# Two more rounding-correction terms in both activation quantizers of a feed-forward sublayer on eight cores

## The reference, cut to what matters

```
def act_quant(x):
    scale = 127.0 / jnp.clip(jnp.max(jnp.abs(x), axis=-1, keepdims=True), 1e-05)
    return jnp.clip(jnp.round(x * scale), -128, 127) / scale
def weight_quant(w):
    scale = 1.0 / jnp.clip(jnp.mean(jnp.abs(w)), 1e-05)
    return jnp.clip(jnp.round(w * scale), -1, 1) / scale
def bit_linear(x, w):        # the value is that of the quantized operands
    return jnp.einsum('bsd,hd->bsh', act_quant(x), weight_quant(w))
...
h = bit_linear(x, w1)                        # 1024 -> 4096
h = silu(depthwise_conv1d(h, conv_w, conv_b))   # 3 taps along the tokens
return bit_linear(h, w2)                     # 4096 -> 1024
```

## Time and profile before

| | |
|---|---|
| time, median of 3 runs | 10609.23 us (10607.76 to 10616.51) |
| the profiled execution: its own time | 10610.17 us |
| its span (slowest core, first to last instruction) | 10608.6 us |
| spans of the 8 cores | 10564.5 to 10608.6 us |
| VectorE busy | 3761.9 us, 35% |
| TensorE busy | 3693.5 us, 35% |
| ScalarE busy | 1905.7 us, 18% |

### The profile page before, as it was taken

The page is one execution under the profiler, slowest core; times in us unless marked ns, Lnnn a source line. Parts: engine busy times, 40 slices in busy tenths (PEclk is TensorE's granted clock), DMA queues, the critical chain, the costliest instruction groups (busy, mean ns, idle before and its releaser), DMA issues.

```text
span 10608.6 us, 72542 instructions; the slowest of 8 cores (10564.5 to 10608.6 us)
## 1 busy us (share of the span) xinstructions
PE 3693.5 (35%) x21474; PEld 2012.1 (19%) x21474; DVE 3761.9 (35%) x6202; ACT 1905.7 (18%) x3771; POOL 0.2 (0%) x4
## 2 busy tenths in 40 slices
PE   3333333400002334443343343333334414433343
PEld 1111111100001222222211111121111102222232
DVE  2111111123357655666411111111111176666655
ACT  1333333000000000000123333333333100000000
POOL 0000000000000000000000000000000000000000
PEclk9555555655555666666665555555555556666666
DMA  1000000032211334333100000000000003333344
GB/s 53 4 4 8 4 5 12 30 97 75 74 51 38 64 75 80 79 80 68 42 2 4 4 1 4 4 1 4 4 4 1 16 2 73 77 79 64 64 86 97
DMA packets 1187213, 407.74 MB, mean 38 GB/s; under 512 B 1129236, under 2 KB 1162264, under 8 KB 1186840
## 3 DMA queue, kind: packets, MB, share of 16 engines
q1 hardware_dynamic: 1186840, 403.11, 17.0%
HBM read 377.88 MB, written 25.17 MB: 38 GB/s over the span
## 4 chain that ended last, share of the span: by engine, by line
PE 30%; DVE 25%; DMA 17%; issue 13%; ACT 10%; DVEq 4%; SPq 1%; ACTq 0%; POOLq 0%
PE ps L43 26%; DVE FQ L43 11%; DMA W1TS<-w1t 7%; DMA WPF<-w 5%; ACT PPBb L43 4%; DVE HQ L43 4%; DVEq L43 3%; DMA W2TS<-w2t 3%; PE pt L43 2%; ACT PPBa L43 2%; DVE LCOL L43 1%; ACT TMPB L43 1%; PE pss L43 1%; DVE TMPA L43 1%; DVE SR L43 1%
## 5 line engine op out<-in xcount | busy, mean ns | idle before, releaser
L43 PE MATMUL ps<-HQ,W2TS 128*128 128x256 bf16 x4096 | 559.5, 304 | 1288.1 <-DVEq L43 1177.9
L43 PE MATMUL ps<-XQT,W1TS 128*128 128x258 bf16 x4096 | 832.1, 376 | 491.1 <-DMA W1TS<-w1t 462.5
L43 PE MATMUL ps<-VBb,PPAb 128*128 128x129 bf16 x2048 | 482.9, 297 | 1003.7 <-ACT PPBb L43 1003.7
L43 DVE RECIPROCAL LCOL<-ps 128x3 f32<-128x3 f32 (+2 forms) x160 | 28.9, 180 | 1982.1 <-PE ps L43 1966.5
L43 PEld LDWEIGHTS ps<-HQ,W2TS 128*128 128x128 bf16 x4096 | 437.1, 109 | 1398.7 <-issue 1308.5
L43 PE MATMUL pt<-CID,TMPB 128*128 128x128 bf16 (+1 forms) x1408 | 183.2, 279 | 1362.9 <-DVEq L43 983.2
L43 PEld LDWEIGHTS ps<-XQT,W1TS 128*128 128x128 bf16 x4096 | 492.8, 128 | 826.0 <-issue 666.0
L43 ACT ACTIVATE PPAb<-ps,LCOL 128x384 bf16<-128x384 f32 (+1 forms) x768 | 418.2, 545 | 995.4 <-PE ps L43 994.8
L43 ACT ACTIVATE TMPB<-ps 128x256 bf16<-128x256 f32 (+1 forms) x192 | 87.3, 454 | 2635.4 <-PE ps L43 2635.4
L43 DVE SCALAR_TENSOR_TENSOR FQ<-ps,CONVP,FQ 128x256 f32<-128x256 f32 x1024 | 495.4, 484 | 82.3 <-issue 6.9
L43 PE MATMUL ps<-VBb,PPBb 128*128 128x129 bf16 x2048 | 519.4, 315 | 0.0
(11 more groups left out here) (139 smaller groups left out, 5491.8 us busy)
## 6 DMA issues: line engine op xcount, KB each, us to landing
W1TS<-w1t SPq DMA_DIRECT2D x512, 256.0 KB, 3.1
W2TS<-w2t SPq DMA_DIRECT2D x128, 1024.0 KB, 7.6
WPF<-w SPq DMA_DIRECT2D x128, 512.0 KB, 4.1
WSAa<-wqkv SPq DMA_DIRECT2D x24, 512.0 KB, 3.9
X<-x SPq DMA_DIRECT2D x1, 8192.0 KB
w1t<-WTS SPq DMA_DIRECT2D x32, 256.0 KB, 2.8
w2t<-WTS SPq DMA_DIRECT2D x32, 256.0 KB, 2.8
out<-X SPq DMA_DIRECT2D x1, 8192.0 KB, 22.0
```

Source lines behind the costliest of these rows:

```text
L43: r = f(*a, **k)
```

## The change

It adds terms to both rounding corrections and touches nothing else. In `qq`, after the comparisons with 0.5, it adds those with 1.5 and 2.5 on either side: four operations over 1024 columns and two drains for each token tile. In `qz` it adds the comparison with 2.5 on either side: two operations over 2048 columns and two drains for each piece, four pieces a chunk. All of it is VectorE work, in place on tiles that exist already; no wait, semaphore, load or matmul is added or moved.

```diff
@@ qq, for each of 16 token tiles
                 v.tensor_single_scalar(FQ[:, 3072:4096], FQ[:, 2048:3072], -0.5,
                                        OP.is_lt)
                 v.drain()
+                v.scalar_tensor_tensor(FQ[:, 0:1024], FQ[:, 2048:3072], 1.5,
+                                       FQ[:, 0:1024], OP.is_gt, OP.add)
+                v.scalar_tensor_tensor(FQ[:, 3072:4096], FQ[:, 2048:3072], -1.5,
+                                       FQ[:, 3072:4096], OP.is_lt, OP.add)
+                v.drain()
+                v.scalar_tensor_tensor(FQ[:, 0:1024], FQ[:, 2048:3072], 2.5,
+                                       FQ[:, 0:1024], OP.is_gt, OP.add)
+                v.scalar_tensor_tensor(FQ[:, 3072:4096], FQ[:, 2048:3072], -2.5,
+                                       FQ[:, 3072:4096], OP.is_lt, OP.add)
+                v.drain()
                 v.tensor_sub(FQ[:, 1024:2048], FQ[:, 0:1024], FQ[:, 3072:4096])
@@ qz, for each of four pieces of a chunk
                     v.scalar_tensor_tensor(B, A, 1.5, B, OP.is_gt, OP.add)
                     v.drain()
+                    v.scalar_tensor_tensor(B, A, 2.5, B, OP.is_gt, OP.add)
+                    v.drain()
                     v.tensor_single_scalar(Ho, A, -0.5, OP.is_lt)
                     v.drain()
                     v.scalar_tensor_tensor(Ho, A, -1.5, Ho, OP.is_lt, OP.add)
+                    v.drain()
+                    v.scalar_tensor_tensor(Ho, A, -2.5, Ho, OP.is_lt, OP.add)
                     v.drain()
                     v.tensor_sub(Ho, B, Ho)
```

## The result

The changed kernel takes 11082.6 us (median of 8 runs, 11058.1 to 11102.0) against 10611.8 us (8 runs, 10604.6 to 10625.2): ratio 1.0441, 95% interval 1.0429 to 1.0452, or +455 to +480 us. The forecast was +460 and 11070, in a range of 11051 to 11091. The profiled execution took 11058.1 us, with a span of 11056.5.

What follows compares the result with a forecast made beforehand. No single engine was taken to bound the kernel, a row of stages in series with VectorE ahead in both touched ones. 10610.17 + 303.4 (qz) + 156.8 (qq) gave 11070.4, stated as 11070 us, range 11,051 to 11,091.

Steps and rivals of the forecast that it cites:

- No single bound, two stages in series: Whole kernel: no engine busy for 36% of the span; in both touched feed-forward stages TensorE waits for VectorE, in series.
- qz, 303.4 us: Hidden-activation stage: two added operations lengthen each of 64 pieces by 4.74 us, 303.4 us in all; lower bound 293.4.
- qq, 156.8 us: Activation stage: two pairs of added operations, 2.45 us each, lengthen 32 tiles by 4.90 us, 156.8 in all; upper bound 166.4.
- rival D: Drains and pairs priced wrongly: qq's in-place 1024-wide operations run apart at 1.30 us, +9.6 us, 11,080; chance 0.10.
- Nothing covers it: Both touched stages: no matmul or weight load can run beside the added VectorE work, so it is paid in full.
- Rival B: W1 and W2 stages run faster and pay back the 460 us; chance 0.01, a small part over 20 us 0.03.
- The clock: TensorE's granted clock is already 0.50 through qz and the activation stage, so a longer rest costs nothing more; 0 taken.
- rival C: TensorE's restart after the longer rest is dearer in the first W2 group and W1 stage, 11,094 to 11,118; chance 0.05.
- Rival A: The added comparisons change no value and do nothing or are dropped, so the time stays 10610; chance 0.01.
- VectorE busy, 4212 us expected: Profile after: VectorE's busy time rises from 3761.9 by 293.4 and 156.9 to 4212 us.
- The period of a chunk, 246.4 us expected: Feed-forward sublayers: the time from one chunk to the next rises from 227.5 to 246.4 us.
- The scatter: Whole time: about 10 us allowed to either side of the bounds, from chunk periods of 227.8 and 227.1 and three runs.

Runs made afterwards that it cites:

- fused: The kernel before, with all comparisons, conversions and subtractions replaced by adding and subtracting 1.5 * 2^23 to round; 9442.4 us against 10579.0, ratio 0.8928.
- qq_only: The kernel before with only the four added operations of qq, qz left as it was; 10740.5 us against 10579.0, ratio 1.0154.
- Pieces: The changed kernel with the first two W2 matmul groups run 8 matmuls behind each qz piece; 11061.9 us against 10613.0 for the kernel before, ratio 1.0430.
- warm run: The changed kernel with 160 unread TensorE matmuls during the last piece of each qz; 11076.9 us against 10613.0 for the kernel before, ratio 1.0443.

## Why the prediction was right

**No single bound, two stages in series.** Right. All of the change shows up as TensorE's wait for VectorE (212.0 to 289.3, 73.4 to 92.7). That the work is exposed was shown from both sides: with VectorE's work made less (fused), the time fell by what the stages lost to within 20 us of 1137, as it rose with more.

**qz, 303.4 us.** It was 306.0, above the 303.4 that I had called the upper bound. The price of an operation held (2.37). The 2.6 more are short stalls of VectorE, put down to "issue". On core 5 the sixteen qz stages have none over 0.15 us before and ten after, 4.3 us in all. They do not hang on the added operations: qq_only has the qz code of before, and its qz stages hold eight stalls and are 2.8 us longer than before. Against it qz grew by 1470.7 - 1167.5 = 303.2. FQ's instructions in the whole program waited 7.3 us in 17 stalls before and 10.8 in 25 after; the row of the change:

```profile
DVE FQ L43 <- issue: 10.8, 25, 0.5
```

The longest is 0.5 us. What they are is not shown. I had left them out; the scatter of the range covered them.

**qq, 156.8 us.** It was 155.6. The upper bound, rival D, fell: the pairs overlap, in place as well. A pair took 4.87 / 2 = 2.44 us, under the 2.45 that was the sign of being wrong.

**Nothing covers it.** Right, within what the trace can tell: W1 and W2 stages moved by -5.2 and -4.8, where the cores of one execution have a standard deviation of 6 to 10. Rival B, that they win back 460, is refuted by this. Pieces tried a cover that can be built in: 49 us in the stages, and nothing that the time could tell from no gain.

**The clock.** Right: it stands at 0.50 through qz before and after, and the first groups' sums, 92.6, 91.9 and 91.7 us behind rests of 73.4, 92.7 and 111.7 us, refute rival C. The Trainium skill (TensorE: Matmul & The Clock Gate, "Why this matters for your kernels") advises to avoid idle gaps between bursts of matmuls. Here the warm run won 15 us in 16 restarts by shortening the gaps to 2.5 us, less than the time can show. The clock had still fallen to 0.50 behind a gap of that length in the first chunk.

**Rival A**, comparisons that do nothing are dropped: refuted, they are in the trace at full price, and the kernel without them is faster by all of it.

**VectorE busy, 4212 us expected.** 4206.3: the overlap of the pairs is counted once (64 pairs by 0.09 = 5.8).

**The period of a chunk, 246.4 us expected.** The amax reductions of the first and the last chunk of the first sublayer, in the chain of the kernel after (core 5):

```profile
3491.16 13.83 DVE FQ L43
...
5224.95 13.83 DVE FQ L43
```

Seven periods of 247.7 us; in the second sublayer 9166.20 to 10871.48 gives 243.6, and the mean of both is 245.6. The earlier trace rows had 227.8 and 227.1, so the two sublayers lie 4 us apart where they had lain 0.7. That is one core: on the mean of the eight, the two periods were 227.7 and 225.8 before and 246.0 and 244.9 after, 18.7 more.

**The scatter.** This is where the prediction was thinnest: I took the scatter of the sum from two means of one core, some 10 us. The stretch ahead of the first activation stage, where all these kernels are the same, ran from 3086.6 to 3127.2 us in the table. The kernel before had a median of 10579.0 us on one chip and 10613.0 on another, and on each its seven executions lie within 30 us. The mean spans differ by 460.6 us, the medians by 470.8. The 10 us between are no more than such scatter, but nothing here shows which stage they lie in. With the median 8 us below the upper end, that the range of 40 us held is in part luck; the mechanism and the prices are not.

## What to carry to other kernels

When one engine waits in one piece for another and nothing else runs meanwhile, each operation of the second costs its start-to-start time in full, as the 2.37 us did here; the count of operations gives the answer. Ask of such a chain which operations are needed at all: here one operation that adds and subtracts a constant did the work of eight that round and correct. To overlap the two engines, split the wait, and first ask which buffer the work done early frees, since the gain here ended at the next load.

## What the runs showed that I had not expected

- An operation with no drain ahead starts 0.08 to 0.09 us before the one before it has ended, at 1024 and at 2048 columns; a drain puts the next start 0.15 to 0.16 us later (2.20 against 2.36). The Trainium skill (VectorE: DVE Perf Modes, "The DRAIN you can't avoid") has the next operation wait until the pipe is empty, but one that it calls not held start earlier. The early starts of the pairs agree with its second part.
- After a rest of 2.5 us behind 20 us of matmuls, the granted clock was 0.50 at the start of a group of 32, which took 5.27 us, not the 3.65 of a group at 1.00.
- VectorE has stalls of up to 0.5 us under "issue". In the qz stages of core 5 there are none before, ten after, and eight in qq_only, where the code of qz is that of before.
- Stages without any edit differ by tens of us from one traced kernel to the next (3086.6 to 3127.2 us ahead of the first activation stage), more than the cores of one execution (a standard deviation of 5 to 10). Part of it may go with the chip: the W1 stages took 1336.6 to 1344.1 us in the four kernels of the first, and 1354.3 to 1360.8 in the four on the second. Compare a change with the kernel before on the same chip.
